# A six-stage transformer kernel on one core: first x block loaded in two parts, one small product moved on TensorE's queue, the turning and splitting of z signalled by feature halves

## The reference

```
x = x + 0.5 * ffn0(layernorm(x))    # RMS norm, dense gelu MLP 256->1024->256 plus 8 experts of 128, top 2
x = x + attn0(layernorm(x))         # relu attention over 256 columns, matrices A, B, C of 32x32, scalar r
x = x + 0.5 * ffn0(layernorm(x))
x = x + 0.5 * ffn1(layernorm(x))    # 8 experts 256->128->256, relu, top 4 with weights 1
x = x + attn1(layernorm(x))         # 16 heads of 16, latent K and V of 128, ALiBi and causal softmax
x = x + 0.5 * ffn1(layernorm(x))
```

## Time and profile before

| | us |
|---|---|
| median of 3 runs | 556.88 |
| lowest and highest of the 3 | 556.08, 559.63 |
| the profiled execution's own time | 557.99 |
| its span, first to last instruction | 556.3 |
| TensorE busy in it | 505.0 (91%) |
| VectorE busy | 390.8 (70%) |
| ScalarE busy | 264.5 (48%) |
| GpSimd busy | 126.7 (23%) |

### The profile page before, as it was taken

One profiled execution on the slowest core, in us unless ns is written; L12 is line 12 of the kernel. 1 busy time (PEld: TensorE's weight loads), 2 busy tenths in 40 slices (PEclk: granted clock), 3 DMA queues, 4 the chain that ended last, 5 costly groups with the idle time before them and its releaser, 6 DMA issues.

```text
span 556.3 us, 9179 instructions
## 1 busy us (share of the span) xinstructions
PE 505.0 (91%) x3074; PEld 428.3 (77%) x3074; DVE 390.8 (70%) x1196; ACT 264.5 (48%) x572; POOL 126.7 (23%) x201
## 2 busy tenths in 40 slices
PE   1999999999999999999999978898579978889996
PEld 1788888888888888888888857786367766668885
DVE  3669786763886754976687878687277777737776
ACT  2657543443334353226553263574446766644441
POOL 1001000110100100100010054365315555414342
PEclk9999999999999999999999997999677999989999
DMA  6332310000000000001100002401627230000011
GB/s 197 94 101 81 95 39 1 0 1 1 2 1 0 2 1 0 2 21 57 39 0 2 1 1 91 108 1 71 193 59 255 80 100 6 0 1 2 1 38 39
DMA packets 16734, 24.83 MB, mean 45 GB/s; under 512 B 2736, under 2 KB 11184, under 8 KB 16592
## 3 DMA queue, kind: packets, MB, share of 16 engines
q1 hardware_dynamic: 15632, 23.73, 14.0%
q10 hardware_dynamic: 1056, 0.51, 0.5%
HBM read 18.99 MB, written 5.24 MB: 44 GB/s over the span
## 4 chain that ended last, share of the span: by engine, by line
PE 78%; issue 6%; DVE 6%; ACT 4%; POOL 4%; DMA 1%; ACTq 1%; DVEq 0%; POOLq 0%
PE ps L575 22%; PE ps L577 21%; PE ps L576 20%; PE ps L893 2%; PE ps L590 2%; DVE x L1597 2%; PE ps L860 2%; PE ps L848 2%; PE ps L879 2%; PE ps L877 2%; POOL al L508 1%; PE ps L966 1%; ACT z L1002 1%; DMA post_b<-in_posts_dram 1%; PE ps L908 1%
## 5 line engine op out<-in xcount | busy, mean ns | idle before, releaser
L575 PE MATMUL ps<-zh,w0u_h 128*128 128x512 f32 x256 | 103.0, 402 | 2.5 <-issue 2.5
L577 PE MATMUL ps<-zl,w0u_h 128*128 128x512 f32 x256 | 102.3, 400 | 0.0
L576 PE MATMUL ps<-zh,w0u_l 128*128 128x512 f32 x256 | 102.0, 398 | 0.0
L1032 ACT ACTIVATE gel<-ps 128x512 f32<-128x512 f32 x64 | 38.3, 598 | 104.1 <-PE ps L577 104.0
L1415 DVE TENSOR_TENSOR act<-gel,ps 128x512 f32<-128x512 f32 x64 | 43.8, 685 | 43.1 <-ACT gel L1032 43.0
L575 PE MATMUL ps<-w0d_h,ah 128*128 128x256 f32 x256 | 73.0, 285 | 0.4
L577 PE MATMUL ps<-w0d_l,ah 128*128 128x256 f32 x256 | 71.4, 279 | 0.0
L576 PE MATMUL ps<-w0d_h,al 128*128 128x256 f32 x256 | 71.4, 279 | 0.0
L508 POOL TENSOR_TENSOR al<-act,ah 128x512 fp32r<-128x512 f32 x32 | 42.2, 1321 | 84.1 <-ACT ah L1109 83.9
L1597 DVE SCALAR_TENSOR_TENSOR x<-ps,aff,x 128x256 f32<-128x256 f32 x128 | 53.0, 477 | 9.9 <-PE ps L577 8.1
L1038 ACT ACTIVATE ah<-act 128x512 fp32r<-128x512 f32 x64 | 40.4, 630 | 40.3 <-DVE act L1415 40.3
(11 more groups left out here) (183 smaller groups left out, 1093.8 us busy)
## 6 DMA issues: line engine op xcount, KB each, us to landing
stage<-in_w_dram SPq DMA_DIRECT2D x16, 384.0 KB, 3.1
q_raw<-split_out SPq DMA_DIRECT2D x24, 128.0 KB, 2.7
k_raw<-split_out SPq DMA_DIRECT2D x48, 64.0 KB, 2.5
stage<-in_w_dram SPq DMA_DIRECT2D x8, 256.0 KB, 2.6
k_raw<-in_zeros_dram SPq DMA_DIRECT2D x1, 1536.0 KB, 11.2
x<-in_x_dram SPq DMA_DIRECT2D x2, 512.0 KB, 5.0
split_out<-qh SPq DMA_DIRECT2D x4, 256.0 KB, 2.1
split_out<-ql SPq DMA_DIRECT2D x4, 256.0 KB, 2.6
```

The costliest lines, as they stand in the source:

```text
L575: pe.matmul(o, lh, rh, start=start, stop=False, **kw)
L576: pe.matmul(o, ll, rh, start=False, stop=False, **kw)
L577: return pe.matmul(o, lh, rl, start=False, stop=stop, **kw)
L1032: nc.scalar.activation(gel[:, n % 2, :], ps[:, 2 * (n % 2), :], ACT.Gelu_apprx_tanh).then_inc(gelu_s, 1)
```

## The change

Three edits. The first norm's block is loaded in two transfers of two tiles each, with a semaphore of its own for the second, and the statistics of tiles 2 and 3 wait for that one. The 32x32 product with its wait for the constants goes from the head of TensorE's list to the place behind unit 1 of the first block and its router product. And transposes, `z_hi` and `z_lo` signal for each feature half, so that zh of half 0 starts after four transposes, and zl of half 0 after zh of half 0; whoever needs both halves waits for twice the count. No arithmetic is added or taken away.

```diff
-        x_in_s = [sem(f"x_loaded{b}") for b in range(2)]
+        x_in_s = [sem(f"x_loaded{b}") for b in range(3)]
...
             def load_x(b):
-                sp.dma_start(x[:, BT * b:BT * (b + 1), :],
-                             x_in[BLK * b:BLK * (b + 1), :].rearrange("(t p) d -> p t d", p=P)).then_inc(x_in_s[b], 16)
+                parts = 1 if b else 2
+                for i in range(parts):
+                    lo, hi = BT * b + BT * i // parts, BT * b + BT * (i + 1) // parts
+                    sp.dma_start(x[:, lo:hi, :], x_in[P * lo:P * hi, :].rearrange("(t p) d -> p t d", p=P))\
+                      .then_inc(x_in_s[2 * i + b], 16)
...
                         mm = pe.transpose(ps[:, kc, t * P:(t + 1) * P], z2[:, NORMS[p][1], t, kc * P:(kc + 1) * P],
                                           ident[:, :])
-                mm.then_inc(zt_s, 1)
+                    mm.then_inc(zt_s, 1)
...
             def split_ready(p):
-                pe.wait_ge(zh_s, zt_count(p))
-                pe.wait_ge(zl_s, zt_count(p))
+                pe.wait_ge(zh_s, KC * zt_count(p))
+                pe.wait_ge(zl_s, KC * zt_count(p))
...
                             logits_t(0, 6, fb == 0)
+                        if fb == 0 and c == 1:
+                            pe.wait_ge(const_s, 16 * N_SETUP)
+                            pe.matmul(ps[0:SA, 7, 0:SA], a0[:, 2 * SA:3 * SA], a0[:, SA:2 * SA], start=True, stop=True)\
+                              .then_inc(pt_ps_s, 1)
...
-            if "attn0" in stages:
-                pe.wait_ge(const_s, 16 * N_SETUP)
-                pe.matmul(ps[0:SA, 7, 0:SA], a0[:, 2 * SA:3 * SA], a0[:, SA:2 * SA], start=True, stop=True)\
-                  .then_inc(pt_ps_s, 1)
             for st in plan:
...
             def z_hi(p):
-                act.wait_ge(zt_s, zt_count(p))
                 for kc in range(KC):
-                    a = nc.scalar.activation(zh[:, kc, :], ps[:, kc, :], ACT.Copy)
-                a.then_inc(zh_s, 1)
+                    act.wait_ge(zt_s, KC * (zt_count(p) - 1) + kc + 1)
+                    nc.scalar.activation(zh[:, kc, :], ps[:, kc, :], ACT.Copy).then_inc(zh_s, 1)
...
                 for t in range(BT):
+                    if p == 0 and t == BT // 2:
+                        dve.wait_ge(x_in_s[2], 16)
                     i = V.bn_stats(bn[:, t, :], x[:, BT * b + t, :])
...
             def z_lo(p):
-                dve.wait_ge(zh_s, zt_count(p))
                 for kc in range(KC):
-                    i = V.tensor_tensor(zl[:, kc, :], ps[:, kc, :], zh[:, kc, :].bitcast(F32), ALU.subtract)
-                i.then_inc(zl_s, 1)
+                    dve.wait_ge(zh_s, KC * (zt_count(p) - 1) + kc + 1)
+                    V.tensor_tensor(zl[:, kc, :], ps[:, kc, :], zh[:, kc, :].bitcast(F32), ALU.subtract).then_inc(zl_s, 1)
```

More of the change, by code:

```diff
@@ L999, in normalise @@
                 act.wait_ge(shift_z_s, p - BY_ACT + 1)
-                act.wait_ge(zt_s, zt_count(last_norm(p)))
+                act.wait_ge(zt_s, KC * zt_count(last_norm(p)))
                 for t in range(BT):
@@ L1313, in normalise @@
                     else:
-                        dve.wait_ge(zt_s, zt_count(last))
+                        dve.wait_ge(zt_s, KC * zt_count(last))
                 for t in range(BT):
```

## The result

| | before | after |
|---|---|---|
| median of 17 runs, us | 558.51 | 555.62 |
| lowest and highest | 555.97, 560.04 | 554.51, 557.21 |
| profiled execution: span, us | 556.3 | 553.6 |
| its mean granted clock | 0.966 | 0.962 |

The ratio is 0.9949, with a 95% interval of 0.9936 to 0.9962: the change takes 2.9 us off, where 4.5 were forecast. The 17 runs of before have a median 1.6 us above that of the three shown ahead of the prediction. So the time of 555.62 lies 3.2 above the forecast 552.4, one half by the gain that is missing and one half by the base, and 0.12 above the stated range.

What follows compares the result with a forecast made beforehand. TensorE, busy for 91% of the span, was taken as the bound, so only its holes count. Opening 2.9 plus attn1's 0.5 and 1.1 made 4.5 us, from 556.88 to 552.4 us, range 549.5 to 555.5.

Steps and rivals of the forecast that it cites:

- The product's wait: Opening: without the 32x32 product's wait for post_b until 10.47 us, transposes start 0.1 us behind z; 1.4 us gained.
- two loads: First x block: first half lands near 3.8 us, second at 4.48; 0.6 us gained, or nothing by the skill page's table.
- Halves: Opening: first product 3.4 us after the first transpose in place of 4.5, starting at 12.1 us; 1.1 us gained.
- The product behind unit 1: The moved 32x32 product costs 0.2 us on TensorE (0.1 to 0.31), and its wait holds up nothing.
- The clock at the opening: Unit 0: the low level lasts 4.6 us of matmuls from the earlier start too, so the whole 2.9 us stays.
- The rival by which the clock rises near 19.8 us whatever TensorE did: Opening: low stretch 3.1 us longer takes back 1.4 us; gain 3.1, 553.8 us; chance 0.17.
- Nothing in the other norms, 0.5 and 1.1 in attn1: Halves gain nothing in ffn0, ffn1 or the score loop's norm; 0.5 us in attn1's first block, 1.1 in its second.
- The rival by which attn1 gives its part back: attn1: reloads through DRAM, or VectorE's adds, end last and not zl; 2.9 us are left, 554.0 us; chance 0.13.
- The sum: Whole kernel: 2.9 us from the opening, 0.5 and 1.1 from attn1, 4.5 us in all, giving a median of 552.4 us.
- a low stretch more: Shifted work meets one more low-clock stretch, 13.2 us long, costing up to 5.9 us: 558.3 us; chance 0.10.
- The bounds: Whole kernel: two loads 0 to 0.7, product 0.1 to 0.31, attn1 0 to 1.6 us, giving gains of 2.2 to 4.8.
- The base: Starting time of the kernel before: 556.88 us, median of three runs; the profiled execution took 557.99 us.

Runs made afterwards that it cites:

- no-loads kernel: The changed kernel with the first x block in one load again, moved product and halves kept: 554.70 us, ratio 0.9957 against the kernel before.
- product alone: The kernel before with only the 32x32 product moved behind unit 1: 557.21 us, ratio 0.9993.
- Before again: The kernel before, unchanged, run for a second trace: 557.36 us, ratio 1.0013.
- halves everywhere: The kernel before with halves at all ten norms, loads and product as before: 555.55 us, ratio 0.9956.
- halves in attn1 alone: The kernel before with halves at the two norms of attn1 only: 556.76 us, ratio 0.9987.
- one filled trace: The changed kernel with unread matmuls in the three holes around attn1's second block and the shortest score matmul issued twice: 552.25 us, ratio 0.9892.
- ordered form: The changed kernel with GpSimd's sixth low part in ffn1's first block made to wait for VectorE's add to x: 555.45 us, ratio 0.9958.
- before, ordered: The kernel before with GpSimd's sixth low part in ffn1's first block made to wait for VectorE's add to x: 557.76 us, ratio 0.9983.
- filled pair: The kernel before and the changed kernel, each with 137 unread matmuls in holes from 330 us on: 557.12 us (0.9992) and 556.36 us (0.9961).
- ordered kernels: The kernel before and the changed kernel, each with GpSimd's low part made to wait for VectorE's add: 557.76 us (0.9983) and 555.45 us (0.9958).

## Why the prediction was right or wrong

*The product's wait and two loads: right at their place.* Forecast: transposes at 8.7; measured 8.85 (9.41, 8.82 and 9.00 in other traces with both edits). The second half of x was counted on at 4.48 and came with its statistics at 4.73: the loads are worth 0.47 (no-loads kernel, 9.32), not 0.6. Over all traces with both edits (8.63 to 9.41, seven) and the two with the moved product and one load (9.23 and 9.32) it is 0.37 in the mean, since the second half arrives anywhere from 4.51 to 5.30. The Trainium skill, page DMA: Bandwidth & Descriptors, section Rules for kernel authors, had spoken against small transfers; at the transposes the trace is nearer to my 0.6 than to the zero that I had estimated from that page's table, and at the end of the program no gain can be measured. One thing was overlooked: post_b, whose wait was taken away, does not land at 10.47 each time. The transposes of the six traces of the table that keep the wait start from 9.92 to 11.16, 10.56 in the mean where 10.71 was reckoned with, so 1.25 of the 1.4 us in the mean.

*Halves: right.* 3.43 us from transposes to product, 3.4 forecast; first product at 12.28, 12.1 forecast.

*The product behind unit 1: right in that nothing waits, its cost too low.* There is no wait and no hole at unit 2. But its row of 0.24 us is not what it costs: the matmuls before and behind it start 0.50 us apart in place of 0.23, and some matmuls later the delay is 0.38 (product alone: 1.44 us ahead of before in front of it, 1.06 behind), where 0.2 was forecast and 0.31 was the bound. Unit 2 starts 3.1 us earlier (21.36 against 24.47), 3.0 are left a few matmuls later, and 2.9 was forecast; that the two agree is in part luck, by what follows.

*The clock at the opening: right in direction, not one for one.* The rise came 3.9 us behind the first product, 4.8 in before, so the low level was 0.9 us shorter and gave 0.4 us, which made up for the product's cost. In the 13 traces without filling the rise came 3.1 to 6.1 us behind the first product, and the step from that product to unit 2 takes 8.8 to 9.9 us. Before again starts its first product 0.45 us earlier than before and unit 2 only 0.02 earlier; halves everywhere starts it 1.88 earlier and unit 2 1.52. The rival by which the clock rises near 19.8 us whatever TensorE did is refuted (15.8 to 16.6 us in the five traces with product and loads, or product and halves); what that rival says of a scatter between its case and mine is borne out.

*Nothing in the other norms, 0.5 and 1.1 in attn1: right.* From unit 2 to 337 us the lead stays at 3.0 us; in attn1 0.42 and 1.08 are gained. Of the 0.55 us ahead of latent K's product 0.27 are left (381.45 comes 0.50 behind the matmul before it, whose like are 0.23 apart). The rival by which attn1 gives its part back is refuted by halves in attn1 alone, where both gains are in the trace of TensorE up to the score loop, and by the unfilled traces, where nothing is given back at the reloads; only in one filled trace 0.6 us were.

*The sum: the step that failed.* "Behind it projections, their splits and the first scores follow one on another, so it is kept." The sum of 4.5 us hands every local gain to the end whole, and puts at nothing, without a reason, what the stretch from 84 to 377 us and the one behind 394 us do with it. 2.9 us arrived (2.4 to 3.1 by means and ratios, over all batches). Two things were seen to take some of it:

- The collision of VectorE and GpSimd. Across 341 us the lead over before fell from 3.4 to 3.0 us in the changed kernel's first trace, from 3.6 to 3.2 in its ordered form, and from 3.1 to 1.6 in its second trace, where GpSimd came first: some 1.1 us more. The product of the second block came 4.6 us earlier in the first trace, but only 3.1 in the second (395.12 against 398.19 in before again). The prediction has no term for this.
- The low clock. Behind the second block's product the same work took 155.2, 154.7 and 154.9 us in the traces of the changed kernel and its ordered form, against 153.3, 154.9 and 155.3 in those of before. That is 0.4 us in the mean, with a spread of 2 us on one side. The rival "a low stretch more" has its mechanism in the first pair of traces, at 1.9 us in place of 5.9; but before, ordered, has the same stretches, so no trace shows that the change brings them, and over all runs the mean clock of the two kernels is the same.

*The bounds.* The terms add up to 2.2 to 4.7; the 4.8 of the prediction is 0.1 too high.

*The base.* 1.6 us of the miss are the three runs on which 556.88 rested. Over all batches before has medians from 557.1 to 558.5, by the groups of the table above; the profiled execution's 557.99 was the better base of the two at hand.

What stays open: how the missing 1.6 us divide between the collision and the low clock, and what part the change has in the latter, whose runs lie more at both ends of the clock table but have the same mean clock. The filled pair, 4.4 us apart where the clock stays up, has neither of the two. The ordered kernels have no collision, and the changed one gained nothing by it, at a lower mean clock. Over three traces of each side (with their ordered forms) the second block's product is 4.3 us earlier in the mean and the last matmul 3.8. That is more than the runs show, because the three traced executions on the side of before took longer than most: 559.3 us in the mean, where the runs of before have 557.9; on the changed side the two means are both 555.5. How often GpSimd comes first in the changed kernel only traces could tell, and there are two.

## What to carry to other kernels

A local gain ahead of a stretch where TensorE is full is kept across it: here 3.0 us over 310 us. It is safe only as far as the schedule's first real holes. Behind these, two things that hang on the moment (which of two engines comes first, where and how long the clock is low) can take or give 1 to 4 us, so forecast such a part as several cases with their weights and not as a shift, and look for them in more than one trace of each kernel before you say that a change brought them. Two traces of before looked like a fixed pattern here, and two of the changed kernel did not. Sort the runs by their mean clock before you compare medians. And where one wait is charged to a load's landing, take its time from several executions before you book what its removal brings: alone, moving the product and splitting the load brought nothing that could be measured, and splitting z's signals by halves, which shortens a chain of three engines, nearly all of the gain.

## What the runs showed of the hardware

- Of two overlapping elementwise instructions on fp32 tensors in SBUF, one of VectorE and one of GpSimd, the second shows up to 1.9 times its length and no idle time, since its wait is booked as busy: GpSimd 1.93 to 2.35 us in place of 1.29, VectorE 2.22 to 2.31 in place of 1.22. The first is not slowed. A start 0.06 us earlier decides.
- At the start of the program TensorE's matmuls of 512 columns start 0.43 us apart and then 0.23; the step came 3.1 to 6.1 us behind the first product in 13 traces, and two traces of one kernel differ in it by 0.9 us.
- The granted clock fell in the same three regions in all six traces of the two kernels and their ordered forms, but two traces of one kernel differ by 3.6 us in where the second of these lies (388 and 392 us), and one of them has two low stretches that the other lacks. Runs of one kernel have mean clocks of 0.960 to 0.971 and times of 555.3 to 560.9 us.
- Matmuls that nothing reads keep the clock up if they fill the holes, and pay only if few are needed: 18 of 512 columns brought 3.7 us (by medians, in the ordered kernel), while 137, 64 of them short, took before from a mean clock of 0.966 to 0.997 and brought nothing.
- Two loads in place of one bring the first half of 512 KB to VectorE 0.8 us earlier (3.58 to 3.76 against 4.32 to 4.58) and the second mostly later (4.51 to 5.30).
